# A transformer-block kernel on one core: order of the first weight pieces, router weights and row statistics in the prologue

## The reference, cut to what matters

```python
x = x + tanh(g_xattn[0]) * xattn0(layernorm(x), ctx, ctx, mask, Wq, bq, Wk, bk, Wv, bv)  # 8 heads
x = x + tanh(g_ffn[0])   * moe(layernorm(x), router_w, gate_w, up_w, down_w)             # 8 experts, top-p 0.9
x = x + tanh(g_xattn[1]) * memory_attention(layernorm(x), ctx, mask_BxS2)
x = x + tanh(g_ffn[1])   * grouped_ffn(layernorm(x), gate_up_proj, down_proj)            # 4 experts
```

## Time and profile before

| | |
|---|---|
| median of 3 runs | 859.29 us (858.58 to 860.84) |
| profiled execution, its own time | 859.4 us |
| its span, first to last instruction | 857.6 us |
| PE busy | 772.9 us, 90% |
| DVE busy | 687.2 us, 80% |
| ACT busy | 595.8 us, 69% |
| POOL busy | 580.2 us, 68% |
| mean granted TensorE clock | 0.958 of full |
| DMA moved | 122.99 MB, mean 143 GB/s |

### The profile page before, as it was taken

The page is one execution under the profiler, slowest core; times in us unless marked ns, Lnnn a source line. Parts: engine busy times, 40 slices in busy tenths (PEclk is TensorE's granted clock), DMA queues, the critical chain, the costliest instruction groups (busy, mean ns, idle before and its releaser), DMA issues. The chain is left out here.

```text
span 857.6 us, 30114 instructions
## 1 busy us (share of the span) xinstructions
PE 772.9 (90%) x11511; PEld 719.4 (84%) x11511; DVE 687.2 (80%) x2385; ACT 595.8 (69%) x1298; POOL 580.2 (68%) x617
## 2 busy tenths in 40 slices
PE   3455689999999999999999999999999999888886
PEld 2343479999999998999999999999999999777875
DVE  3576778888888888888888888888888886898973
ACT  3267768877787877787887878787878773454442
POOL 4255637788879797979797888888888674222321
PEclk9657689999999999999999999999999999999999
DMA  7579999879998989898898889897888864120002
GB/s 234 166 146 235 237 230 206 149 140 158 150 162 143 156 150 148 157 142 161 147 172 138 167 138 165 137 176 143 152 153 154 128 107 135 51 63 14 26 4 97
DMA packets 319540, 122.99 MB, mean 143 GB/s; under 512 B 274716, under 2 KB 312612, under 8 KB 319396
## 3 DMA queue, kind: packets, MB, share of 16 engines
q1 hardware_dynamic: 318656, 120.53, 73.5%
q10 hardware_dynamic: 740, 0.54, 0.2%
HBM read 45.53 MB, written 8.39 MB: 63 GB/s over the span
## 5 line engine op out<-in xcount | busy, mean ns | idle before, releaser
L591 POOL TENSOR_TENSOR p_parts<-p,p_parts 128x512 f16<-128x512 f32 x256 | 296.7, 1159 | 114.3 <-ACT p_parts L706 103.2
L846 PE MATMUL psG<-xT,w_gu 128*128 128x128 f16 x3072 | 193.5, 220 | 7.2 <-DVE th_ga_h L1282 6.8
L583 POOL TENSOR_TENSOR hp_lo<-th_ga_h,hp_hi 128x512 f16<-128x512 f32 x136 | 157.7, 1160 | 57.2 <-ACT hp_hi L728 54.0
L846 PE MATMUL psU<-xT,w_gu 128*128 128x128 f16 x3072 | 192.2, 219 | 1.4 <-DVE th_ga_h L1290 1.3
L846 PEld LDWEIGHTS psG<-xT,w_gu 128*128 128x128 f16 x3072 | 176.3, 98 | 11.9 <-DVE th_ga_h L1282 9.7
L846 PE MATMUL psY<-w_dn,hp_hi 128*128 128x256 f16 x1024 | 181.7, 273 | 0.8 <-POOL hp_lo L583 0.8
L846 PEld LDWEIGHTS psU<-xT,w_gu 128*128 128x128 f16 x3072 | 175.4, 98 | 3.2 <-DVE th_ga_h L1290 2.6
L706 ACT ACTIVATE p_parts<-p 128x512 f16<-128x512 f32 x256 | 160.6, 627 | 6.1 <-DMA p_turn<-p_parts 5.6
L1206 DVE CUSTOM_DVE_ANT_0 ps<-ps,mask_in 128x256 f32<-128x256 f32 x256 | 104.2, 448 | 55.2 <-PE ps L846 54.6
L698 ACT ACTIVATE p<-ps,exp_bias 128x256 f32<-128x256 f32 x256 | 106.9, 469 | 48.1 <-DVE exp_bias L1210 46.8
L846 PE MATMUL psY<-w_dn,hp_lo 128*128 128x256 f16 x512 | 139.6, 273 | 0.0
(11 more groups left out here) (180 smaller groups left out, 1089.5 us busy)
## 6 DMA issues: line engine op xcount, KB each, us to landing
mask_in<-in_mask_Bx2048x_ff SPq DMA_DIRECT2D x32, 256.0 KB, 3.0
part_scratch<-parts SPq DMA_DIRECT2D x16, 384.0 KB, 4.0
q_stack<-part_scratch SPq DMA_DIRECT2D x62, 96.0 KB
k_stack<-part_scratch SPq DMA_DIRECT2D x62, 96.0 KB
stage<-in_L_ffn_gate_w SPq DMA_DIRECT2D x8, 512.0 KB, 4.4
stage<-in_L_ffn_up_w SPq DMA_DIRECT2D x8, 512.0 KB, 4.4
stage<-in_L_ffn_down_w SPq DMA_DIRECT2D x8, 512.0 KB, 4.4
p_turn<-p_parts SPq DMA_TRANSPOSE x256, 3.7
```

Source lines behind the costliest of these rows:

```text
L583: pool.tensor_tensor(hp_lo[:, u % 2, :], hb32[:, u % 2, :], hp_hi[:, u % 2, :], ALU.subtract).then_inc(s["h_split"], 1)
L591: pool.tensor_tensor(p_parts[:, g % 4, 1, :, :], p32[:, g % 2, :, :], p_parts[:, g % 4, 0, :, :], ALU.subtract).then_inc(s["plo_done"], 1)
L846: return pe.matmul(out_, lhsT, rhs, start=start, stop=stop, skip_group_check=shares_bank)
```

## The change

Four things move, and nothing is added or removed.

1. Pieces 0 and 1 (`W_FRONT` = 2): PE turns them right behind `project_qk(0, 0)` and ahead of `project_v(0, 0)`. ACT takes their high parts behind `norm1(1)` and ahead of `copy_qk(1)`. DVE takes their low parts at the same place as before, right behind the memset of `q_stack`. Pieces 2 to 5 keep their place on PE and ACT.
2. The router's two transposes on PE go ahead of `project_qk(1, 1)`; DVE's four instructions on `w_rt` go ahead of the low parts of pieces 2 to 5.
3. The row statistics of the prologue go ahead of the low parts of pieces 2 to 5 too, and are eight rows instead of six (`STATS_AHEAD` = 10). Step 0 then does pairs 10 to 15 in groups 0 to 2, and none in group 3.
4. DVE's wait for `consts_ready` goes to the end of the prologue.

```diff
-STATS_AHEAD = 8
+STATS_AHEAD = 10
+W_FRONT = 2
@@ scalar
             norm1(1)
+            for w in range(W_FRONT):
+                w_high(w // 6, w % 6 // 2, w % 2)
             copy_qk(1)
             for piece in range(2, 4):
                 load_stacks(act, 0, 0, piece)
-            for w in range(W_AHEAD):
+            for w in range(W_FRONT, W_AHEAD):
                 w_high(w // 6, w % 6 // 2, w % 2)
@@ tensor
             project_qk(0, 0)
+            for w in range(W_FRONT):
+                weight_transposes(w // 6, w % 6 // 2, w % 2)
             pe.wait_ge(s["qk_copied"], 2)
             project_v(0, 0)
-            pe.wait_ge(s["v_copied"], 1)
-            project_qk(1, 1)
-            for w in range(W_AHEAD):
-                weight_transposes(w // 6, w % 6 // 2, w % 2)
             pe.wait_ge(s["rt_loaded"], 16)
             for k in range(KT):
                 last = pe.transpose(psY[:, 0, k * NE:k * NE + NE], rt_in[:, k * P:k * P + P], ident[0:NE, 0:NE])
             last.then_inc(s["router_T"], 1)
+            pe.wait_ge(s["v_copied"], 1)
+            project_qk(1, 1)
+            for w in range(W_FRONT, W_AHEAD):
+                weight_transposes(w // 6, w % 6 // 2, w % 2)
@@ vector
             dve.memset(q_stack[:, 1, :, :, :, :], 0.0).then_inc(s["q_zeroed"], 1)
-            for w in range(W_AHEAD):
+            for w in range(W_FRONT):
                 w_low(w // 6, w % 6 // 2, w % 2)
-            dve.wait_ge(s["consts_ready"], 5)
             dve.wait_ge(s["router_T"], 1)
             for k in range(KT):
                 ...
             dve.wait_ge(s["x_loaded"], 16)
             norm1_stats(2, STATS_AHEAD)
+            for w in range(W_FRONT, W_AHEAD):
+                w_low(w // 6, w % 6 // 2, w % 2)
+            dve.wait_ge(s["consts_ready"], 5)
```

## The result

The changed kernel takes **854.51 us** (median of 8 runs, 850.53 to 856.80) where the kernel before takes 859.21 (8 runs, 858.32 to 861.44): ratio 0.9937, 95% interval 0.9915 to 0.9959. By the ratio that is 5.4 us; 853.5 with a range of 851.7 to 857.2 was predicted. The profiled execution took 856.54 us, its span is 854.8, so this one profile shows only 2.8 us of gain and has to be read with care.

What follows compares the result with a forecast made beforehand. It took DVE's order in the prologue, 6.5 us idle and then a 5.3 us queue, as the bound. Gain 6.2 - 0.1 (stacks) - 0.3 (c = 4) = 5.8, so 859.3 - 5.8 = 853.5 us, range 851.7 to 857.2.

Steps and rivals of the forecast that it cites:

- Low parts 0 and 1 without a wait, from 20.56: On DVE in the prologue: both run right behind the memset, 1.4 us in all, to 21.95.
- Early pieces on PE cost nothing: On PE in the prologue: two pieces take 1.94 us, project_v(0, 0) ends at 17.7, its reader began at 18.00.
- Statistics to 28.2, low part 2 behind them: On DVE in the prologue: eight rows take 5.44 us to 28.2, 1.15 us past where low part 2 could begin.
- `maxima(0)` at 32.3, bound 0.9 us later by the stacks, 0.1 taken: End of the prologue: maxima(0) at 32.3 instead of 38.56, gain 6.2 us; stack landings cost 0 to 0.9, 0.1 taken.
- New wait in group 0 for piece 6, 0.95 us: Step 0: DVE waits 0.95 us because piece 6 needs c = 3; the two extra statistics rows pay for it.
- c = 4 issued earlier, 0.3 us: SP issues c = 4 near 27.1 instead of 29.86, sharing DMA engines with c = 3; up to 3.2 us, 0.3 taken.
- Group 4 at 44.0, gain 6.2, less 0.4 for DMAs: Group 4 begins at 44.0 instead of 50.27; 0.1 for stacks and 0.3 for c = 4 come off the gain.
- Everything behind shifts as a whole: After group 4: same order, tied by semaphores to DVE's groups, so work up to 110 us and the experts shift whole.
- Rival A: c = 3, stacks or first transposing DMAs are delayed, eating 2 to 3 us of the gain: about 856.0; chance 0.18.
- Rival B: DMA backlog fixed in time sets the early steps' pace; gain under 2.6 us, about 858.5; chance 0.09.
- Rival C: PE's clock rises late as experts begin 5.8 us earlier; gain gone after some 12 us, 863.5 with 20; chance 0.04.
- Rival D: PE or ACT reaches pieces 0 and 1 too late, so DVE's order stays as long: about 859.3; chance 0.03.

Runs made afterwards that it cites:

- the third profile: The changed kernel, unaltered, profiled and timed a third time: median 854.3 us, ratio 0.9935 to the kernel before.
- the second: The changed kernel, unaltered, profiled and timed again: median 854.2 us, ratio 0.9933 to the kernel before.
- second profile of before: The kernel before, with no edit, profiled a second time: the execution took 862.5 us.
- busy-PE pairs: Four fp32 matmuls, result unused, added on PE in each of groups 18 to 29: changed kernel 853.4 us; filled 851.4 to 850.2; before 859.4 to 858.2.
- statistics only: Changed kernel with only statistics and router weights moved, all six pieces behind as before (W_FRONT = 0): 855.0 us, ratio 0.9939 to before.
- filled: Changed kernel with its statistics spread into DVE's remaining gaps: 853.0 us, ratio 0.9918 to before; run again, 851.4 us, ratio 0.9902.

## Why the prediction was right, point by point

- *Low parts 0 and 1 without a wait, from 20.56.* Right: 20.21. The DVE order of this execution ran 0.27 us ahead from the start.
- *Early pieces on PE cost nothing.* Right: `project_qk(0, 0)` was done some 0.5 us earlier, the two pieces took 1.7 us instead of the 1.94 of the earlier trace rows, and `project_v(0, 0)` ended at 16.2, well ahead of its reader at 17.73.
- *Statistics to 28.2, low part 2 behind them.* 27.57. Right but for the 0.6 us by which DVE was ahead.
- *`maxima(0)` at 32.3, bound 0.9 us later by the stacks, 0.1 taken.* Measured 32.69. The stacks were the bound that counted: `scores(0)` waited 1.55 us for them to 31.90, so the term was 0.8 to 0.9 and not 0.1. In the third profile they were there at 31.10, in the second by 30.25, where `scores(0)` began without a wait. DVE, 0.6 us ahead of the sum, was free at 31.7 and stood idle 0.98 us for the scores.
- *New wait in group 0 for piece 6, 0.95 us.* 1.02. In other profiles 0.76 and 1.14. The sum missed a second one: DVE stood idle 0.35 us more ahead of `maxima(1)`, with no other engine named, so from group 0 to group 1 it was 4.36 us and not 3.95. Group 3 took 1.57 instead of 1.82, which gave 0.25 us of that back.
- *c = 4 issued earlier, 0.3 us.* Not shown. c = 3 landed 6.9, 5.6 and 6.0 us after its issue in the three profiles of the changed kernel, and 6.4 and 7.1 in the two of before.
- *Group 4 at 44.0, gain 6.2, less 0.4 for DMAs.* 44.48, gain 5.8; in the other two profiles 7.0 and 6.4. The path was right and the sum close, in part because its errors cancel: the stacks and the wait of 0.35 us cost more than it said, DVE's lead and group 3 gave it back. That it hit 5.8 exactly in the first profile is chance, as the landings of the stacks and of c = 3 move by over a microsecond from run to run.
- *Everything behind shifts as a whole.* Right until the experts, 6.35 us at 110.42. By the medians 5.4 to 5.8 us arrive at the end, against 5.8 to 7.0 at group 4, so at most about 1 us is given back. Over all kernels the two columns of the table follow each other from 2.2 to 9.2 us.
- *Rival A, the gain partly eaten.* c = 3 did not land later, see above. But the first profile looks like A: 2.8 us of gain at its end, after a wait for a transposing DMA. The medians, 5.4 to 5.8 us, and the second profile of before speak against it as the rule.
- *Rival B, DMA engines as the clock of the early steps.* Their share was over 1 from 70 to 120 us in before (1.07) and after (1.12), and yet the start of the experts moved by all that was won. Ruled out: a busy DMA stretch whose loads are all released by the groups moves with them.
- *Rival C, the clock.* Its rise did shift with the work (full from 107.6 instead of 113.5, by the granted clock of the stretches), and it fell again in a 3 us wait, which was in none of my cases. In the changed kernel this cost a part of the 2.7 us lost between groups 29 and 34 in the first profile; the busy-PE pairs put all that their matmuls mend, the half clock included, at about 1 us in the median. To undo the gain of 5.8 us it would have to be some five times as large. The rule of the Trainium skill ("TensorE: Matmul & The Clock Gate", "What's actually happening") that activity releases the clock agrees with the rise at 107.6, ahead of which PE had been busy throughout from 104.07.
- *Rival D, the gap is not filled.* Low part 0 began right behind the memset, so D is out.
- *What would make it wrong: the stretch from group 4 to the experts.* 110.53 - 51.17 = 59.4 before and 104.19 - 45.38 = 58.8 after (`exp_bias` of groups 4 and 26). Not longer.

What the title of the change promised most, the two early pieces, adds least: undone, it costs 0.4 to 0.7 us in the median, inside the spread. The parts do not add up, though. The pieces alone won 2.8 us, statistics and router weights alone 5.2, both together 5.4 to 5.8: they fill the same idle stretch, and with both in it the landings of the stacks and of c = 3 set the pace.

Open: whether the added matmuls help by the clock or by keeping the long wait away; what stops the DMA engines for a microsecond near group 29, and whether the change makes it more frequent. Two profiles of before, three of the changed kernel and one or two of each variant are too few, and no kernel was made to stop it.

## What to carry to other kernels

Where one engine idles early and is the last to be waited for a few microseconds later, move into the gap whatever needs only data already there; it arrives at the end in full if everything behind is released by that engine's groups, however busy the DMA engines are. Then write down which landing is next in line: here the stacks and c = 3 capped the gain, turning two pieces early as well added under 1 us, and spreading the rest of the statistics over the waits that these landings made was worth another 1.2 to 2.8 us. Differences of 1 to 3 us between two profiles of a kernel like this are chance; judge by marks inside the profile and by medians at the end.

## What the runs showed of the hardware that I had not expected

- All 16 DMA engines at once moved next to nothing for 1 us or more, with a transposing DMA under way. In the second profile of before it is the same, 116.5 to 119.5 us in slices of 0.075 us:

```profile
DMA  9469009000000010000000009999969696990090
```

- PE's clock fell from full to half in a wait of 3.2 us, and the next 6.9 us ran at 0.51: there the wait was paid for twice. This is not so each time. Waits of 2.7 us (second profile of before), 3.7 us (statistics only) and 2.6 us (filled) left the clock full, and the next half expert took 1.50 us.
- The long middle repeats in steps of 20.0 and 20.8 us, from group 4 to group 4, but in 7 of the 14 profiles one step takes 1.0 to 2.1 us more. In the changed kernel's first profile it was one of 22.5 us, ended at 390 us, in which PE waited 1.57 us for a transposing DMA:

```profile
373.02 0.36 PE L849 MATMUL psV<-v_parts,p_turn 128*128 128x25 bf16 x8 [1.57 <-DMA p_turn<-p_parts]
```

  Together with the wait near group 30 this accounts for the 3.1 us between the two profiles of before; that it makes up the spread of some 6 us among the timed runs (850.5 to 856.8) is likely but not shown.
